# Last head pair and drain of a two-layer block: earlier weight folds, probabilities on GpSimd, outputs ahead of the gate and up products

## What is computed

```python
def _L1_xattn_ref(query, key, value, mask, wq, wk, wv, wo, curr_seq_pos):
    ...
    q = _apply_rope(q, curr_seq_pos)
    k = _apply_rope(k, curr_seq_pos)
    raw = jnp.einsum('bhqd,bhkd->bhqk', q, k) / scale
    attn = jax.nn.softmax(masked, axis=-1)
    out = jnp.einsum('bhqk,bhkd->bhqd', attn, v)
    return out @ wo
def _L1_ffn_ref(x, w_gate, s_wgate, w_up, s_wup, w_down, s_wdown, inv_gate, inv_up, inv_inter):
    ...
    qg, sg = _dynamic_quant(x_flat, inv_gate)
    qu, su = _dynamic_quant(x_flat, inv_up)
    gate_out = _quant_gemm(qg, sg, w_gate, s_wgate)
    up_out = _quant_gemm(qu, su, w_up, s_wup)
    inter = jax.nn.silu(gate_out) * up_out
    inter = jnp.clip(inter, -SWIGLU_LIMIT, SWIGLU_LIMIT).astype(jnp.bfloat16)
    qi, si = _dynamic_quant(inter, inv_inter)
    out = _quant_gemm(qi, si, w_down, s_wdown)
x = x + jnp.tanh(g_xattn[1]) * _L1_xattn_ref(_layernorm(x), ctx_4096, ctx_4096, mask_BxSxS2_ff0, ...)
x = x + jnp.tanh(g_ffn[1]) * _L1_ffn_ref(_layernorm(x), ...)
```

## Time and profile before

| | us |
|---|---|
| median of 3 runs (lowest, highest) | 847.76 (847.03, 848.78) |
| the profiled execution | 845.51 |
| its span | 843.7 |
| TensorE matmuls busy | 774.3 (92%) |
| VectorE busy | 662.9 (79%) |
| GpSimd busy | 380.9 (45%) |
| ScalarE busy | 352.3 (42%) |

### The profile page before, as it was taken

The page is one execution under the profiler, slowest core; times in us unless marked ns, Lnnn a source line. Parts: engine busy times, 40 slices in busy tenths (PEclk is TensorE's granted clock), DMA queues, the critical chain, the costliest instruction groups (busy, mean ns, idle before and its releaser), DMA issues.

```text
span 843.7 us, 12571 instructions
## 1 busy us (share of the span) xinstructions
PE 774.3 (92%) x4276; PEld 613.4 (73%) x4276; DVE 662.9 (79%) x1230; ACT 352.3 (42%) x1064; POOL 380.9 (45%) x324
## 2 busy tenths in 40 slices
PE   2898998888989999999999999999999999969975
PEld 1565565786867788888878888877888787757754
DVE  5788888888978877778788777787877778798972
ACT  2777776221334333333333333434333243237541
POOL 2787787415364433333253332434423333386541
PEclk9999999897999999999999999999999999989995
DMA  8310030101021111011020100102101020200101
GB/s 256 107 51 25 25 106 0 39 0 51 1 76 50 38 38 51 26 38 39 26 63 26 51 26 26 48 29 63 38 26 38 26 88 24 55 4 1 38 25 38
DMA packets 37460, 37.43 MB, mean 44 GB/s; under 512 B 2912, under 2 KB 27232, under 8 KB 37408
## 3 DMA queue, kind: packets, MB, share of 16 engines
q1 hardware_dynamic: 35184, 32.81, 13.3%
q10 hardware_dynamic: 2224, 3.94, 1.5%
HBM read 34.64 MB, written 2.10 MB: 44 GB/s over the span
## 4 chain that ended last, share of the span: by engine, by line
PE 63%; DVE 6%; POOL 4%; issue 3%; ACT 2%; POOLq 0%; DVEq 0%; ACTq 0%
PE QB L1478 6%; PE QB L1480 6%; PE SB L1598 6%; PE QB L1479 6%; PE ROW L1479 6%; PE ROW L1478 6%; PE ROW L1480 6%; PE KV L1478 4%; PE PB L1571 3%; PE KV L1479 3%; PE KV L1480 3%; DVE rope_b L1244 2%; PE KV L1662 2%; PE TB L1541 2%; POOL dense L976 1%
## 5 line engine op out<-in xcount | busy, mean ns | idle before, releaser
L976 POOL TENSOR_TENSOR dense<-rope_a,rope_b 128x512 f32<-128x512 f32 x62 | 79.4, 1280 | 167.5 <-DVE rope_b L1244 167.3
L1110 ACT ACTIVATE ot_hi<-PB 128x512 fp32r<-128x512 f32 x64 | 38.3, 599 | 198.4 <-PE PB L1571 198.2
L1101 ACT ACTIVATE e_sb<-masked,nmax 128x64 f32<-128x64 f32 x256 | 86.1, 337 | 58.1 <-DVE nmax L1273 57.7
L1478 PE MATMUL QB<-xT_hi,wq_lo 128*128 128x512 f32 x256 | 107.0, 418 | 0.0
L1479 PE MATMUL ROW<-wo_lo,ot_hi 128*128 128x512 f32 x256 | 101.7, 397 | 0.0
L1480 PE MATMUL QB<-xT_hi,wq_hi 128*128 128x512 f32 x256 | 101.7, 397 | 0.0
L1479 PE MATMUL QB<-xT_lo,wq_hi 128*128 128x512 f32 x256 | 101.5, 396 | 0.0
L1478 PE MATMUL ROW<-wo_hi,ot_lo 128*128 128x512 f32 x256 | 101.3, 396 | 0.0
L1480 PE MATMUL ROW<-wo_hi,ot_hi 128*128 128x512 f32 x256 | 101.0, 395 | 0.0
L1241 DVE TENSOR_TENSOR rope_a<-QB,rope 128x512 f32<-128x512 f32 x62 | 42.8, 691 | 72.7 <-PE QB L1480 72.5
L1282 DVE TENSOR_TENSOR p_sb<-e_sb,rz 128x256 f32<-128x256 f32 x64 | 86.8, 1356 | 2.2
(11 more groups left out here) (200 smaller groups left out, 1902.2 us busy)
## 6 DMA issues: line engine op xcount, KB each, us to landing
raw<-in_wq SPq DMA_DIRECT2D x32, 256.0 KB, 2.7
raw<-in_wo SPq DMA_DIRECT2D x32, 256.0 KB, 2.6
ctx_two<-in_ctx SPq DMA_DIRECT2D x16, 256.0 KB, 3.8
x_sb<-in_x SPq DMA_DIRECT2D x8, 256.0 KB, 7.1
...
```

What stands on the lines that cost most here:

```text
L976: nc.gpsimd.tensor_tensor(dst, a, b, ALU.add).then_inc(s_rot, 1)
L1101: nc.scalar.activation(e_sb[:, r, :], masked[:, r, :], ACT.Exp, bias=nmax[:, r:r + 1], accum_out=zsum[:, r:r + 1]).then_inc(s_exp, 1)
L1478: nc.tensor.matmul(out, lhs[1], rhs[0], start=first, stop=False)
```

## The change

Four edits, all in `last` of the engines:

- The gate and up weights lie over the first half of the columns of the transposed x (`xt_hi`, `xt_lo`), which the query product of step 7 reads last. They are folded in steps 7 and 8, rounded on ScalarE in 8 and 9, and subtracted in 8 and 9. The down weights are folded in step 10, rounded and subtracted in 11.
- In steps 12 to 15 VectorE only takes the inverse of the sum (`inverse`), and GpSimd multiplies (`probabilities`).
- In steps 16 and 17 TensorE runs `outputs` and `weighted` first and `gate_up` behind them; from step 16 on `down` stands behind `gate_up`. The bodies of VectorE for steps 16 and 17 are written out in a new order, and GpSimd takes the last `inverse_deviation` at the same step but ahead of its clips.
- From step 16 on `down` writes by turns to the banks `SB` and `PB`, which the scores and weighted values no longer use, and waits accordingly (`down_bank`).

```diff
@@ -886,7 +886,7 @@
         wd_raw = [c["wd_raw"][:, k, :] for k in range(IC)]
-        wgu = [[x[:, n, :].rearrange("p (k i) -> p k i", k=KC) for n in range(2)] for x in (ctx_hi, ctx_lo)]
+        wgu = [[x[:, :, INNER * n:INNER * n + INNER] for n in range(2)] for x in (xt_hi, xt_lo)]
         wd = [[x[:, 2, D * k:D * k + D] for k in range(IC)] for x in (ctx_hi, ctx_lo)]
@@ -894,7 +894,12 @@
         xi = [rope_b[:, INNER * p:INNER * p + INNER] for p in range(2)]
-        TQ, GU, TI, DN = QB, KV, TB, QB[1]
+        TQ, GU, TI = QB, KV, TB
+        def down_bank(t):
+            return QB[1] if t + DOWN < SLOTS else (SB_, PB2[:, 0, :])[t % 2]
         LAST = PAIRS - 1
@@ -1055,6 +1060,12 @@
 
+            def probabilities(N):
+                pool.wait_ge(s_rz, N + 1)
+                pool.wait_ge(s_t, N - 1)
+                nc.gpsimd.tensor_tensor(p_sb[:, N % 2, :, :], e_sb[:, :, :],
+                                        rz[:, :].unsqueeze(2).broadcast_to([P, 4, S]), ALU.mult).then_inc(s_p, 1)
             def last():
@@ -1068,26 +1079,28 @@
                         fold_rows()
+                    if n in (7, 8):
+                        fold_gate_up(n - 7)
                     if n in (8, 9):
-                        fold_gate_up(n - 8)
+                        weight_rest(n - 8, wgu[1][n - 8], wgu_raw[n - 8], wgu[0][n - 8])
                     if n == 10:
-                        weight_rest(0, wgu[1][0], wgu_raw[0], wgu[0][0])
+                        for k in range(IC):
+                            fold_down(k)
                     if n == 11:
                         for k in range(IC):
-                            fold_down(k)
-                    if n == 12:
-                        for k in range(IC):
                             weight_rest(2 + k, wd[1][k], wd_raw[k], wd[0][k])
+                    if 12 <= n < SLOTS:
+                        probabilities(SLOTS * LAST + n)
+                    if n == SLOTS + 1:
+                        inverse_deviation(nc, pool, c, s_var, s_rstd, 7, 8, 10)
                     if (t := ffn_tile(n, INTER)) is not None:
...
                         inner_smooth(t)
-                    if (t := ffn_tile(n, STATS)) is not None:
+                    if n <= SLOTS and (t := ffn_tile(n, STATS)) is not None:
                         inverse_deviation(nc, pool, c, s_var, s_rstd, t, t + 1, 3 + t)
-                    if n == 10:
-                        weight_rest(1, wgu[1][1], wgu_raw[1], wgu[0][1])
 
@@ -1195,12 +1208,12 @@
                         exps(N)
-                    if n == 10:
+                    if n in (8, 9):
+                        act.wait_ge(s_q, SLOTS * LAST + 12)
+                        act.wait_ge(s_fold, n - 5)
+                        nc.scalar.activation(wgu[0][n - 8], wgu_raw[n - 8], ACT.Copy).then_inc(s_fhi, 1)
+                    if n == 11:
                         act.wait_ge(s_k, 4 * PAIRS)
-                        for i in range(2):
-                            act.wait_ge(s_fold, 3 + i)
-                            nc.scalar.activation(wgu[0][i], wgu_raw[i], ACT.Copy).then_inc(s_fhi, 1)
-                    if n == 12:
                         for k in range(IC):
@@ -1272,6 +1285,11 @@
                   .then_inc(s_max, 1)
+            def inverse(N):
+                dve.wait_ge(s_exp, 4 * N + 4)
+                dve.wait_ge(s_p, N)
+                nc.vector.reciprocal(rz[:, :], zsum[:, :]).then_inc(s_rz, 1)
 
@@ -1431,7 +1449,7 @@
                 dve.wait_ge(s_dn, t + 1)
-                nc.vector.scalar_tensor_tensor(out=x_sb[:, t, :], in0=DN[:, :], scalar=sci[:, t % 2:t % 2 + 1],
+                nc.vector.scalar_tensor_tensor(out=x_sb[:, t, :], in0=down_bank(t)[:, :], scalar=sci[:, t % 2:t % 2 + 1],
                                                in1=x_sb[:, t, :], op0=ALU.mult, op1=ALU.add).then_inc(s_x, 1)
@@ -1444,24 +1462,46 @@
                         rope_q(q_job(LAST, n), N + 4, n % 4)
-                    if (t := ffn_tile(n, INTER)) is not None:
-                        inner_scales(t)
-                    if (t := ffn_tile(n, DOWN)) is not None:
-                        add_down(t)
-                    if (t := ffn_tile(n, SMOOTH)) is not None:
-                        scales(t)
-                    if n < SLOTS:
-                        normalize(N)
-                    if (t := ffn_tile(n, GATE)) is not None:
-                        inner(t)
-                    if n <= SLOTS + 1:
+                    if n <= SLOTS:
+                        if (t := ffn_tile(n, INTER)) is not None:
+                            inner_scales(t)
+                        if n < SLOTS and (t := ffn_tile(n, DOWN)) is not None:
+                            add_down(t)
+                        if (t := ffn_tile(n, SMOOTH)) is not None:
+                            scales(t)
+                        if n < 12:
+                            normalize(N)
+                        elif n < SLOTS:
+                            inverse(N)
+                        if n < SLOTS and (t := ffn_tile(n, GATE)) is not None:
+                            inner(t)
                         accumulate(N - 2, (n - 2) % 8)
-                    if (t := ffn_tile(n, STATS)) is not None:
-                        stats(t)
-                    if n <= SLOTS:
+                        if (t := ffn_tile(n, STATS)) is not None:
+                            stats(t)
                         rest_ot(N - 1)
-                    if (t := ffn_tile(n, STATS)) is not None:
-                        to_bf16(t)
+                        if n == SLOTS:
+                            inner(4)
+                        if (t := ffn_tile(n, STATS)) is not None:
+                            to_bf16(t)
+                        if n == SLOTS:
+                            add_down(2)
+                    elif n == SLOTS + 1:
+                        inner_scales(4)
+                        accumulate(N - 2, 7)
+                        stats(7)
+                        inner(5)
+                        to_bf16(7)
+                        scales(6)
+                        add_down(3)
+                    else:
+                        if (t := ffn_tile(n, INTER)) is not None:
+                            inner_scales(t)
+                        if (t := ffn_tile(n, SMOOTH)) is not None:
+                            scales(t)
+                        if (t := ffn_tile(n, GATE)) is not None:
+                            inner(t)
+                        if (t := ffn_tile(n, DOWN)) is not None:
+                            add_down(t)
                     if n in K_SLOTS and n < 12:
@@ -1641,7 +1681,7 @@
                     pe.wait_ge(s_parts, 3 * q_job(LAST, 11) + 3)
-                if t >= 3:
+                if t in (3, 4):
                     pe.wait_ge(s_x, t - 2)
@@ -1677,12 +1717,15 @@
                     pe.wait_ge(s_flo, 4)
-                pe.wait_ge(s_qt, 2 * min(t + 3, TILES))
-                if t > TILES - 3:
-                    pe.wait_ge(s_x, t)
+                if t + DOWN < SLOTS:
+                    pe.wait_ge(s_qt, 2 * t + 6)
+                elif t < 4:
+                    pe.wait_ge(s_masked if t % 2 == 0 else s_otlo, SLOTS * PAIRS)
+                else:
+                    pe.wait_ge(s_x, t - 1)
                 for k in range(IC):
                     for h in (1, 0):
-                        mm = nc.tensor.matmul(DN[:, :], qi_t[:, k, :], wd[h][k],
+                        mm = nc.tensor.matmul(down_bank(t)[:, :], qi_t[:, k, :], wd[h][k],
                                               start=(k == 0 and h == 1), stop=(k == IC - 1 and h == 0))
@@ -1700,16 +1743,26 @@
                         query(QB[n % 2][:, :], (n // 4 + 1) % 2, n % 4)
-                    if (t := ffn_tile(n, DOWN)) is not None:
-                        down(t)
-                    if (t := ffn_tile(n, GATE)) is not None:
-                        gate_up(t)
-                    if n <= SLOTS + 1:
+                    if n < SLOTS:
+                        if (t := ffn_tile(n, DOWN)) is not None:
+                            down(t)
+                        if (t := ffn_tile(n, GATE)) is not None:
+                            gate_up(t)
                         outputs(N - 2)
-                    if (t := ffn_tile(n, INTER)) is not None:
-                        inner_transposes(t)
-                    if n <= SLOTS:
+                        if (t := ffn_tile(n, INTER)) is not None:
+                            inner_transposes(t)
                         weighted(N - 1)
+                    else:
+                        if n <= SLOTS + 1:
+                            outputs(N - 2)
+                        if n == SLOTS:
+                            weighted(N - 1)
+                        if (t := ffn_tile(n, GATE)) is not None:
+                            gate_up(t)
+                        if (t := ffn_tile(n, DOWN)) is not None:
+                            down(t)
```

(3 more changed lines are left out.)

## The result

The changed kernel is **slightly slower**: 849.65 us median of 20 runs (845.34 to 851.52) against 846.70 us for the kernel before in 20 runs (844.13 to 848.78). The ratio is 1.0026 with a 95% interval of 1.0016 to 1.0037, which is 2.2 us more (1.4 to 3.1). The forecast was 0.9 us more, in a range of 845.5 to 851.9.

The account below looks back on a forecast made before the run. Bound in the last 125 us: a 9.02 us loop from `gate` through `clip` and transposes to `gate_up`. Weights -1.3, probabilities 0, drain giving that back, net +0.9 on 847.76: 848.7 us, range 845.5 to 851.9.

Parts of the forecast that it names:

- Step 8: VectorE's `normalize` is held up by GpSimd's earlier fold, delaying two transposes on TensorE: +0.8 us, bounds 0 and 1.2.
- `to_bf16` of tile 0: In step 10 the second GpSimd subtraction is gone, so this VectorE operation takes 0.55 instead of 2.61 us: -2.06 us.
- Part 1 as a whole: Weights folded earlier: -1.3 us in sum, with the transposes of step 15 moving from 794.58 to 793.3 us.
- Part 2: Probabilities on GpSimd in steps 12 to 15: VectorE wins time, but outside the loop that sets the steps, so 0 us.
- rival 3: VectorE was the bound in steps 12 to 15, so moving the probabilities gives its full gain: 846.2 us, chance 0.09.
- Step 17, clock high: Step 17 was reckoned at 1.1 + 2.9 + 2.1 us from its transposes, so `gate_up(5)` ends at 810.1 us.
- rival 1: The clock falls one step earlier, so `outputs` and the rest of step 17 run at half speed: +2.8, 851.5 us, chance 0.22.
- Scales of tile 6: In step 17 `scales(6)` now stands behind `inner(5)` and `to_bf16(7)` on VectorE: 3.7 us later, the transposes of that tile +3.3.
- Last `gate_up`: In step 19, with the low clock taken and `down` now behind, this point comes at 833.6 against 832.70 us: +0.9.
- The drain as one term: The new order from step 16 on uses up the 1.3 us gained earlier and leaves the end 0.9 us later.
- Rival 2: The drain costs nothing: step 8's multiply precedes the fold, clock high from tile 7's transposes on: 845.7 us, chance 0.13.
- rival 4: GpSimd becomes the bound in steps 12 to 15, 0.6 us in each of four steps: 851.1 us, chance 0.06.

Follow-up runs that it names:

- e1: The changed kernel with the drain and probabilities of the kernel before, so only the weights earlier: ratio 0.9980 to the kernel before, 1.7 us faster.
- e4: The changed kernel with `scales(6)` moved ahead of `stats(7)`, `inner(5)` and `to_bf16(7)` on VectorE in step 17: ratio 0.9991 to the kernel before.
- e9: The changed kernel with extra matmuls, result unread, where TensorE stands still in the drain: ratio 0.9977 to the kernel before, 1.9 us faster.
- e2: The changed kernel without the drain's edits, so weights earlier and probabilities on GpSimd: 843.48 us, ratio 0.9955 to the kernel before.
- e3: The kernel before with the drain's edits alone: ratio 1.0059 to the kernel before, 5.0 us slower.
- e11: The kernel before with one edit, the probabilities of steps 12 to 15 on GpSimd: ratio 0.9974 to the kernel before, 2.2 us faster.

## Why the prediction was right in total and wrong in two of its terms

The time, the sign and the reason (the drain gives back what the weights win) were right. Two terms were wrong, the gain of the probabilities and the price of the drain, and they went opposite ways; that the total came out this well is in part luck.

- **Step 8, +0.8**: the transposes wait 0.39 us and the scores of step 10 come 0.58 us later. Mechanism right, size near, and lower in every trace: the transposes wait 0.38 to 0.55 us where the fold goes first. What the forecast had covered by a query, ScalarE's rounding ahead of `round_ot`, is not covered: it costs 0.3 to 0.5 us where the multiply goes first.
- **`to_bf16` of tile 0, -2.06**: 0.55 us instead of 2.61. The first transposes are at +37.82; 755.2 and the 0.8 of step 8 is +38.1 in this count. The wait ahead of them is 4.75 us, forecast 4.6.
- **Part 1 as a whole, -1.3** at the transposes of step 15: -1.9 in the changed kernel, -1.7 us in e1's time. Step 12 won more than the 0.25 of the forecast, since its 0.84 us wait went entirely (the transposes of tile 1 come 2.4 us earlier), of which 0.5 was given back by step 14.
- **Part 2, 0**: wrong. It is worth 2.2 us alone (0.9 to 3.5) and 2.1 on top of the weights; the traces place 0.85 to 0.9 of it between tiles 4 and 5. The failed step is "outside the loop". The loop of steps 12 to 14 is indeed closed without VectorE, and rival 3 is wrong there. But the earlier trace rows have the transposes of tiles 4 and 5 at 794.58 and 804.45, 9.87 and not 9.02 us apart, with an 0.86 us wait, and the forecast left that one distance unexplained. The earlier trace rows have its cause: the maximum of tile 5 waits for GpSimd's smoothing, which waits for `to_bf16`.
- **Step 16**: from the transposes of tile 4 to those of tile 5 are 10.95 us, forecast 10.7. Right.
- **Step 17, clock high**: partly wrong. In this execution the low level lies from 807 to 811 us over the transposes and `outputs`, so that `gate_up` of tile 5 ends 7.3 us behind the transposes, not 6.1. This is rival 1's mechanism, which the forecast gave 0.22: it comes in 6 of 7 executions with `outputs` first and costs 1.5 us against e4's trace (5.8 us), not 2.8, since it ends within the step. The forecast's 6.1 was 0.3 too long for the high level.
- **Scales of tile 6, 3.7 us later**: 4.5 us later; the low stretch, 1.2 us over the forecast's 6.1, more than covers the difference. The transposes of tile 6: +4.0, forecast +3.3; the wait ahead of them is 4.56, forecast 4.7, and the low level over tile 6 came as forecast. e4 takes away the late scales and wins 3.0 us; e9 takes away the low level and wins 4.1. The two overlap and don't add up, for e4 also has its transposes of tile 6 at the high level (1.09 us).
- **Last `gate_up`, +0.9**: +1.9 (+116.64 against +114.77). The extra 1.0 us is there at the transposes of tile 7 already (+4.0, forecast +3.0). "From there the order is the same" missed that the clock need not be: the rest takes 9.96 us against 11.02, most of it at the high level, and the end is +0.81. So the +0.81 of the trace meets the +0.9 of the forecast by two errors of about 1 us that cancel.
- **The drain as one term**: the forecast has it at 0.9 + 1.3 = 2.2 us over the old one; alone it costs 5.0 and on top of the other two parts 6.0. The sum came out because the drain was reckoned from absolute rows to the end of the changed kernel, while what the old drain would have made of the earlier steps never entered: e2's shows 3.8 us, with no low level until tile 7. The forecast of the changed kernel stood, the forecast of its parts did not.
- **Rival 2 and rival 4**: the drain isn't free (e3), and no `clip` waits for the probabilities: in e11 the multiply ends 0.8 us ahead of it.
- **The chances**: the terms for slower add up to 0.41 and those for the same to 0.42, where 0.40 and 0.43 stand. Nothing hangs on it.

Why the 20 runs say +2.2 us and the two traces +0.8 stays open. A possible reason is that the profiled execution of before has its low clock stretches placed badly: its median, less the 2 us around the span and a mean start of step 8 at 720.9, gives an end near +124 as an estimate, not the +125.8 of the trace. The same reckoning gives +126.7 for the changed kernel, and its trace has +126.6. Beside the experiments the kernel before had medians of 847.4 to 847.7 us, which give +125, so the estimate is good to 1 us at best. No run here tests that.
